# First layer of a graph network: the transposed one-hot rows made by ScalarE from destination numbers instead of turned by TensorE

## The reference, cut to what matters

```python
k = typed_linear(x, Wk, ntype, 3).reshape(n, H, D)      # q, v likewise
k_e = k[src]; v_e = v[src]; q_e = q[dst]
...
a = (kw * q_e).sum(-1) * pri[etype] / sqrt(D)            # 8 heads
attn = softmax of a over the edges of each dst
h = segment_sum(mv * attn[..., None], dst, num_segments=n)
h = typed_linear(h.reshape(n, H * D), Wa, ntype, 3)
x = layernorm(x + h * alpha + x * (1 - alpha))
# second layer: msg = (x @ weight[rel])[src] * norm * gate, summed by dst, relu, layernorm
```

## Time and profile before

| | us |
|---|---|
| median of 3 runs | 1799.43 (1798.69 to 1802.08) |
| the profiled execution | 1795.05 |
| its span | 1793.4 |
| PE busy | 1320.5 (74%) |
| DVE busy | 922.8 (51%) |
| POOL busy | 888.6 (50%) |
| ACT busy | 493.5 (28%) |

### The profile page before, as it was taken

The page is one execution under the profiler, slowest core; times in us unless marked ns, Lnnn a source line. Parts: engine busy times, 40 slices in busy tenths (PEclk is TensorE's granted clock), DMA queues, the critical chain, the costliest instruction groups (busy, mean ns, idle before and its releaser), DMA issues.

```text
span 1793.4 us, 21502 instructions
## 1 busy us (share of the span) xinstructions
PE 1320.5 (74%) x6758; PEld 1086.3 (61%) x6758; DVE 922.8 (51%) x1914; ACT 493.5 (28%) x1069; POOL 888.6 (50%) x905
## 2 busy tenths in 40 slices
PE   5789999558999999999999999932454444444445
PEld 4788888447878787878787878721233233233224
DVE  5734445457777777777777777320322222222222
ACT  3222322304454545454545454510000000000000
POOL 1041000375565656565656563057566666666662
PEclk9899999768999999999999999965566666666667
DMA  7454446565676767776767675343333333333332
GB/s 143 134 147 135 138 132 229 156 194 171 209 237 209 239 207 236 212 238 210 239 208 240 208 239 169 109 114 105 88 104 103 105 103 104 103 104 102 102 103 63
DMA packets 103851, 286.56 MB, mean 160 GB/s; under 512 B 20805, under 2 KB 40409, under 8 KB 100661
## 3 DMA queue, kind: packets, MB, share of 16 engines
q0 software_dynamic: 56032, 169.34, 31.9%
q1 hardware_dynamic: 47774, 116.71, 21.3%
HBM read 189.33 MB, written 96.65 MB: 159 GB/s over the span
## 4 chain that ended last, share of the span: by engine, by line
PE 57%; issue 24%; DVE 7%; DMA 6%; POOL 3%; ACT 1%; SPq 1%; another core or an unknown queue 1%; DVEq 0%; ACTq 0%; POOLq 0%
PE bank L954 15%; PE bank L837 11%; PE bank L865 10%; PE bank L729 5%; PE bank L795 5%; DMA kv_table<-tstage 4%; PE bank L783 2%; PE bank L751 2%; PE bank L737 2%; POOL kv L651 2%; PE bank L813 1%; DVE kv L1367 1%; DVE S L1372 1%; POOL kv L637 1%; PE bank L757 1%
## 5 line engine op out<-in xcount | busy, mean ns | idle before, releaser
L637 POOL DMA_INDIRECT kv<-kv_table,rows x416 | 457.8, 1101 | 306.6 <-PE bank L865 132.5
L651 POOL DMA_INDIRECT kv<-message_table,rows x416 | 394.8, 949 | 266.5 <-issue 122.8
L954 PE MATMUL bank<-kv,onehot_w 128*121 128x256 f32 x832 | 274.4, 462 | 334.1 <-issue 292.5
L954 PEld LDWEIGHTS bank<-kv,onehot_w 128*121 128x121 f32 x832 | 185.0, 224 | 423.6 <-issue 395.5
L837 PE MATMUL bank<-wr_r,x1T_r 128*121 128x512 f32 x1248 | 323.2, 401 | 2.2 <-ACT mstage L1098 2.2
L837 PEld LDWEIGHTS bank<-wr_r,x1T_r 128*121 128x121 f32 x1248 | 216.6, 183 | 51.4 <-ACT mstage L1098 3.4
L1504 DVE SCALAR_TENSOR_TENSOR z<-bank,xb 121x256 f32<-121x256 f32 x26 | 10.9, 418 | 414.9 <-remote 304.6
L1098 ACT ACTIVATE mstage<-bank,gate 121x256 f32<-121x256 f32 x416 | 171.4, 471 | 149.4 <-PE bank L837 133.6
L865 PE MATMUL bank<-kv,onehot_r 128*121 128x264 f32 x832 | 203.4, 393 | 0.0
L1176 ACT ACTIVATE sd<-mv,eps 121x1 f32<-121x1 f32 x26 | 7.7, 295 | 600.3 <-DVE mv L1510 513.4
L865 PEld LDWEIGHTS bank<-kv,onehot_r 128*121 128x121 f32 x832 | 150.9, 187 | 29.4
(11 more groups left out here) (135 smaller groups left out, 1396.7 us busy)
## 6 DMA issues: line engine op xcount, KB each, us to landing
message_table<-mstage SPq DMA_DIRECT2D x104, 484.0 KB
kv_table<-tstage SPq DMA_DIRECT2D x26, 1210.0 KB
kv<-kv_table,rows POOLq DMA_INDIRECT x416
kv<-message_table,rows POOLq DMA_INDIRECT x416
query_table<-qstage_r SPq DMA_DIRECT2D x26, 242.0 KB
qb_r<-query_table SPq DMA_DIRECT2D x26, 242.0 KB
kv<-in_Wr POOLq DMA_DIRECT2D x2, 2048.0 KB, 14.5
xb<-in_x SPq DMA_DIRECT2D x26, 121.0 KB
```

Source lines behind the costliest of these rows:

```text
L637: pool.indirect_dma_start(kv[:, n % 2, u, 0:2 * C], None, ktab, bass.IndirectOffsetOnAxis(ap=rows[:, 0, n, u:u + 1], axis=0)).then_inc(kv_ ...
L651: pool.indirect_dma_start(mrows[:, r.q, u, :], None, mtab, bass.IndirectOffsetOnAxis(ap=rows[:, 1, r.number, u:u + 1], axis=0)).then_inc(l ...
L954: last = mm(b_l[r.q][:NODES, 0:C], onehot_w[:, r.q, u, :], mrows[:, r.q, u, :], start=(u == 0), stop=(u == U - 1))
```

## The change

`onehotT_r` is no longer made from `onehot_r`. In every round SP reads the round's 2048 destination numbers, one line of 8 KB, into each of 121 partitions (`dsts`, 968 KB in all). For a group of four units ACT computes |destination - own node| in place (`apart`: Abs with a bias for each partition), and then relu(1 - that) into `onehotT_r` (`mark`), which is 1 where they agree and 0 elsewhere. The edges lie in `dsts` in memory order, so `onehotT_r` has its unit index innermost: the 128 columns of one unit's stationary operand are now 64 bytes apart, and each ACT operation takes 512 elements in runs of four. The 16 turns of a round on PE and the four ACT copies are gone.

```diff
                 onehot_r = msb("onehot_r", [P, 2, U, NODES], F32R)
-                onehotT_r = msb("onehotT_r", [NODES, U, P], F32R)
+                with ExitStack() as dst_life:
+                    dsts = sb("dsts", [NODES, P, U], I32, dst_life)
+                onehotT_r = msb("onehotT_r", [NODES, P, U], F32R)
...
+            def load_dst(r):
+
+                if not r.first:
+                    sp.wait_ge(qe_ready[1], r.nth(QB, 0))
+                s = sp.value_load(starts[0:1, bass.ds(r.number, 1)], min_val=0, max_val=E)
+                sp.dma_start(dsts[:, :, :].rearrange("n p u -> n (p u)"),
+                             dst_lines[0:1, bass.ds(s, ROUND_EDGES)].to_broadcast([NODES, ROUND_EDGES])
+                             ).then_inc(dst_landed, 16)
...
                 if not r.final:
                     load(r.next())
+                    load_dst(r.next())
...
-            def turn_onehot(r, g):
-                if g == 0:
-                    pe.wait_ge(oh_ready, r.done)
-                if g:
-                    pe.wait_ge(ohT_ready[g - 1], r.done)
-                else:
-                    wait(pe, ohT_ready[G - 1], r.number)
-                for q in range(GU):
-                    last = mm(b_ohT[:NODES, q * P:(q + 1) * P], onehot_r[:, r.par, g * GU + q, :], ident_r[:, :],
-                              start=True, stop=True)
-                last.then_inc(ohT_filled[g], 1)
...
-                            last = mm(b_qe[pr % 2][:, q * C:(q + 1) * C], onehotT_r[:, 2 * pr + q, :],
+                            last = mm(b_qe[pr % 2][:, q * C:(q + 1) * C], onehotT_r[:, :, 2 * pr + q],
...
-                    turn_onehot(n, 0)
                 messages(4)
                 if n:
-                    turn_onehot(n, 1)
                     hand_queries(n, 0)
...
-            def keep_onehotT(r, g):
-                act.wait_ge(ohT_filled[g], r.done)
-                a(onehotT_r[:, g * GU:(g + 1) * GU, :], b_ohT[:NODES, :].rearrange("p (a b) -> p a b", a=GU),
-                  ACT.Copy).then_inc(ohT_ready[g], 1)
+            def apart(r, g):
+
+                if g == 0:
+                    act.wait_ge(dst_landed, r.stores())
+                d = dsts[:, :, g * GU:(g + 1) * GU]
+                a(d.bitcast(F32), d, ACT.Abs, bias=minus_id[:NODES, bass.ds(r.number, 1)]
+                  ).then_inc(far_ready, 1)
+
+            def mark(r, g):
+                act.wait_ge(far_ready, r.nth(G, g + 1))
+                u = slice(g * GU, (g + 1) * GU)
+                a(onehotT_r[:, :, u], dsts[:, :, u].bitcast(F32), ACT.Relu, scale=-1.0, bias=1.0).then_inc(ohT_ready[g], 1)
...
                 messages(2)
+                if n:
+                    apart(n, 0)
                 messages(3)
                 if n:
-                    keep_onehotT(n, 0)
+                    mark(n, 0)
+                    apart(n, 1)
                 exps(r)
                 if n:
-                    keep_onehotT(n, 1)
+                    mark(n, 1)
```

More of the change, by code:

```diff
@@ L189, in build @@
         ident = sb("ident", [P, P])
-        ident_r = sb("ident_r", [P, P], F32R)
         iota_n = sb("iota_n", [P, NODES])
         base = sb("base", [P, ROUNDS])
+        minus_id = sb("minus_id", [P, ROUNDS])
         nmask = sb("nmask", [P, TILES, NT])
@@ L294, in build @@
         b_l = (bank[0], bank[1], bank[2], bank[4])
-        b_qe, b_ohT, b_agg, b_tmp, b_out, b_m = bank[0:2], bank[2], bank[3], bank[4], bank[5], bank[6:8]
+        b_qe, b_agg, b_tmp, b_out, b_m = bank[0:2], bank[3], bank[4], bank[5], bank[6:8]
         ld_grid, ld_x, ld_wa, ld_wr, ld_gw, ld_rel, ld_small, ld_rec = (sem(n) for n in (
@@ L303, in build @@
             "rel_high", "rel_low", "wr_high", "wr_low", "gw_high", "gw_low"))
-        const_ready, zeroed, rel_ready, ident_high = (sem(n) for n in (
-            "const_ready", "zeroed", "rel_ready", "ident_high"))
+        const_ready, zeroed, rel_ready = (sem(n) for n in ("const_ready", "zeroed", "rel_ready"))
         pool_step = sem("pool_step")
@@ L317, in build @@
         kv_landed = [sems(f"kv_landed{p}_", G) for p in range(2)]
-        ohT_filled, ohT_ready = sems("ohT_filled", G), sems("ohT_ready", G)
+        dst_landed, far_ready, ohT_ready = sem("dst_landed"), sem("far_ready"), sems("ohT_ready", G)
         qe_ready, qe_used = sems("qe_ready", 2), sems("qe_used", 2)
@@ L504, in l0 @@
                     store_x1(r.last())
+            load_dst(Round(sp, 0, 0))
             load(Round(sp, 0, 0))
@@ L598, in _ @@
             pool.iota(base[:, :], pattern=[[NODES, ROUNDS]], base=0, channel_multiplier=0,
+                      allow_small_or_imprecise_dtypes=True)
+            pool.iota(minus_id[:, :], pattern=[[-NODES, ROUNDS]], base=0, channel_multiplier=-1,
                       allow_small_or_imprecise_dtypes=True)
@@ L862, in aggregate @@
                 if g == 0:
+                    pe.wait_ge(oh_ready, r.done)
                     wait(pe, hN_ready, r.number)
@@ L896, in l0 @@
                 turn_back(r)
-                if n:
-                    turn_onehot(n, 0)
                 messages(4)
                 if n:
-                    turn_onehot(n, 1)
                     hand_queries(n, 0)
@@ L909, in l0 @@
                 if n:
-                    turn_onehot(n, 2)
                     hand_queries(n, 1)
@@ L914, in l0 @@
                 aggregate(r, 2)
-                if n:
-                    turn_onehot(n, 3)
                 aggregate(r, 3)
@@ L922, in _ @@
             first = Round(pe, 0, 0)
-            for g in range(G):
-                turn_onehot(first, g)
             for g in range(G - 1):
@@ L1012, in _ @@
             act.wait_ge(const_ready, 1)
-            a(ident_r[:, :], ident[:, :], ACT.Copy).then_inc(ident_high, 1)
             act.wait_ge(ld_gw, 16)
@@ L1141, in l0 @@
                     keep_x1T(f)
+                if n:
+                    apart(n, 2)
                 messages(5)
                 if n:
-                    keep_onehotT(n, 2)
+                    mark(n, 2)
+                    apart(n, 3)
                 if f:
@@ L1147, in l0 @@
                 if n:
-                    keep_onehotT(n, 3)
+                    mark(n, 3)
                 messages(6, 7)
@@ L1151, in _ @@
             for g in range(G):
-                keep_onehotT(Round(act, 0, 0), g)
+                apart(Round(act, 0, 0), g)
+                mark(Round(act, 0, 0), g)
                 if g % 2 == 0:
@@ L1353, in _ @@
             dve.wait_ge(x_low, STEPS * NX)
-            dve.wait_ge(ident_high, 1)
             v.memset(den[:, :], 1.0).then_inc(tables_over, 1)
```

## The result

| | us |
|---|---|
| before, median of 4 runs | 1799.06 (1797.53 to 1802.08) |
| after, median of 4 runs | 2025.66 (2022.81 to 2032.71) |
| ratio after / before | 1.1263, 95% interval 1.1244 to 1.1281 |
| forecast | 1909, range 1835 to 1985 |
| span of the profiled execution after | 2024.6 (before 1793.4) |

What follows compares the result with a forecast made beforehand. PE was taken to set the pace, with ACT's wait for the late `dsts` costing more than PE saves: 23 rounds at 3.2 and 1.2 us (74 + 28), plus 6 and 2, make 110; 1909 us, range 1835 to 1985.

Steps and rivals of the forecast that it cites:

- R: The beginning of a round on ACT's timeline; in the kernel before, rounds are 29.82 us apart.
- E: The start of `exps` on ACT; in the kernel before 12.49 us after R, with the next R 17.33 later.
- the case with nothing late: Rival: `dsts` lands in time for ACT, a round is 28.7 us, total 1775 to 1780; chance 0.08.
- I take R + 14.5, between them.: Landing of the `dsts` load, chosen between bounds R + 12.0 and R + 16.1; rounds 3.2 us longer.
- the upper bound, R + 16.1: Latest landing of `dsts`: 10.7 us, from the queue's 1.16 MB in 10 us with stores queued beside gathers.
- The estimate from the Trainium skill: 121 rows over 11 of 16 DMA engines: `dsts` takes 12 us, lands at R + 17.5, rounds 6.2 us more.
- I take the first for PE, since it is PE's own: PE's weight loads from columns 64 bytes apart cost nothing extra, by 8-column loads of 87 ns either way.
- The bound from ACT's row: Strided weight loads at ACT's 0.93 ns an element: 119 ns more a load, 2.85 us a round.
- The rival with both mechanisms: Late `dsts` load and dear strided weight loads on PE together: 66 us more, 1975 us; chance 0.22.
- E to the next round: From `exps` to the next round's beginning: 15.85 us instead of 17.33, DVE's products limiting PE's saving.
- 1.2 for the clock: PE's lower clock after its gap waiting for `mark`: 1.2 us a round, bounds 0 and 4.3.
- The cover: The store behind `dsts`, awaited by ACT's message 4: cost nothing while covered, 1 to 2 us a round otherwise.

Runs made afterwards that it cites:

- e9: Changed kernel with some data left out, `dsts` in its own buffer and loaded a round ahead, operand columns side by side, 121 partitions: 1796.83 us, 0.9990 of the kernel before.
- e8: Changed kernel with some data left out, `dsts` in its own buffer and loaded a round ahead, columns side by side, 128 partitions: 1781.67 us, 0.9891 of the kernel before.
- e4: Changed kernel with `dsts` read into 128 partitions instead of 121, all data computed: 1943.93 us, 1.0791 of the kernel before.
- e1: Kernel before, turns still on PE, with only the change's layout of `onehotT_r` (columns 64 bytes apart): 1877.17 us, 1.0423 of the kernel before.
- e6: Changed kernel with some data left out, `dsts` in its own buffer and loaded a round ahead, columns 64 bytes apart: 1827.30 us, 1.0143 of the kernel before.
- e5: Changed kernel with some data left out and `dsts` in its own buffer, load still late, columns 64 bytes apart: 2015.22 us, 1.1211 of the kernel before.
- e7: Changed kernel with some data left out and `dsts` in its own buffer, load still late, columns side by side: 2024.41 us, 1.1266 of the kernel before.
- e12: Kernel before, some data left out, plus the `dsts` load at the change's place ahead of the message stores, unused: 1976.49 us, 1.0976 of the kernel before.
- e3: Changed kernel with the `dsts` load issued ahead of the query and x rows: 1978.99 us, 1.0982 of the kernel before.
- e13: Kernel before, some data left out, plus the unused `dsts` load between the third and fourth message store: 1807.15 us, 1.0022 of the kernel before.
- e11: Kernel before, columns still side by side, but ACT's copy written in steps of 512 bytes: 1802.90 us, 1.0021 of the kernel before.

## Why the prediction failed

**Right.** The wait and its place, ACT at line 1053 ahead of message 3 with `exps` behind it, and the turns' removal lost in it. The issue at R + 5.4 was met to 0.1 us. `mark` took 626 ns against 634 forecast, `apart` 716. From the landing to `exps` 2.5 us passed (2.7). PE's busy share fell to 84% (some 80 forecast), its clock to 0.91. From E to the next R, with nothing late and the columns together, 15.85 us were worked out and e9 has 16.3. For the case with nothing late I had 1775 to 1780; e8 took 1781.67, but that is in part luck, since it leaves data out and has the columns together and 128 rows.

**Step that failed first: the landing.** "I take R + 14.5, between them." Measured R + 18.25 in the round above and R + 17.7 in the mean of rounds 3 to 23. Even the upper bound, R + 16.1, was below every one of these rounds. From issue to use I had bounds of 6.6 and 10.7 us; 128 rows stay within them (9.0 in e4), the 121 of the change don't (12.4). Both bounds came from transfers of another shape, and neither carried over. The estimate from the Trainium skill ("DMA: Bandwidth & Descriptors", the section on why a DMA increments its semaphore by 16), 12 us and R + 17.5, which the sum did without, was the nearest. The miss is 3.2 us a round. The first load, too, took longer than the 8.1 us assumed. Its issue and landing at the layer's start, 10.7 us apart, on SP's queue and on ACT:

```profile
342.20 0.38 SPq L493 DMA_DIRECT2D dsts<-in_dst_lines  x1
```

```profile
352.88 0.72 ACT L1053 ACTIVATE dsts<-dsts,minus_id 121x512 f32<-121x512 int32 x1 [21.58 <-DMA dsts<-in_dst_lines]
```

The layer begins 12.9 us later, where 6 were taken.

**Step that failed second: "I take the first for PE, since it is PE's own".** The row of PE's own load covers 8 columns, too few to show what 128 show. The bound from ACT's row was right almost to the number for a load: 119 ns more estimated, 122 measured in e1. Its 2.85 us a round, for three groups between E and the next R, were too much: at that place the columns cost 1.3 to 1.6 us (e6 to e9, e5 to e7). The rival with both mechanisms, at 1975, was the nearest case. That the columns were cheap was wrong, then, but with the load late it isn't shown to have cost the change anything: e7 has them together and is no faster than e5.

**E to the next round**, 15.85 and 1.2 for the clock forecast, 19.66 measured (853.20 to 872.86): 2.6 more; 19.3 and 2.3 more in the mean. I had DVE's products as what comes last, with group 2's sums at E + 7.7. They start at E + 10.65 (863.85), because PE comes late: queries, message 5 and the sums before them end at E + 8.2 (861.42) instead of E + 6.5. Both the slower loads and the lower clock are in that. The six message matmuls, 2.90 against 1.63, are 1.3 us of it, at a clock of 0.50, and have nothing to do with the columns. Nor have most of the first eight query matmuls, 2.16 us: with the columns together e7 has 2.07 for them. The second eight, 2.03 against 1.17 at a clock of 1.00, are the columns'. By the table of e5, e6, e7 and e9, the 15.85 were 0.5 too low, and the 1.2 for the clock, a guess between 0 and 4.3, 0.1 to 0.4; the columns, put at nothing, are the large part with 1.3 to 1.6.

**The sum.** 33.05 + 1.2 = 34.25 us a round forecast. 3.2 for the landing, 2.3 from E on and 0.2 less up to E make the 39.5 of rounds 3 to 23. Against the forecast that is 110 us in these 21 rounds. The first round begins 7 us later than was allowed for, and 4 us are lost behind the last round. Some 5 come off, since the forecast put 4.4 us between profile and median, where the profiled run after lies 0.6 above its median. That is, to 1 us, the 117 by which the forecast was short. e4 is a test of the sum with the landing nearly as it was put: used at R + 14.3, it still took 1943.93 us, 35 more than 1909. Its rounds 3 to 23 take 36.2 us, and what they have too much stands behind E (19.4 instead of 17.05). So some 80 us of the miss go with the landing and some 35 with what follows E.

**The cover.** "I cost it at nothing; with that cover gone it is 1 to 2 us a round." In the change the cover stands, so this is no part of the miss. But the price without it was wrong: 7.1 us a round in e12. A mend of the landing alone, without a word on the store behind it, can find this wait next, as e3 did; e4, with a shorter load and the same landing, has no such wait in its list.

## What to carry to other kernels

A large load costs by what it stands ahead of. Before placing one in a queue, list for each transfer behind it who waits for that and when: the same bytes cost 176 us ahead of a store that is waited for (e12) and 3 us behind it (e13). When a wait for a load goes, look for the second wait that it hid, and for the lower clock that the gap had brought. Don't take the price of a strided operand from a narrow instruction: here 8 columns showed nothing of what 128 cost, and the worse row of another engine was the better guess.

## What the runs showed of the hardware that was not expected

- A weight load of 128 fp32 columns from 121 partitions: 190 ns with columns side by side, 197 at 8 bytes from one to the next, 327 at 16, 312 at 64. With 8 columns it was 87 at 4 and at 64 bytes alike.
- 8 KB into each of 121 partitions took 11.0 to 13.7 us from issue to use (mean 12.4), into 128 partitions 7.9 to 10.0 from the same queue (mean 9.0) and 8.8 to 10.9 from another engine's (mean 10.0).
- With PE idle for 7.3 us in a round of the change, its granted clock was 0.50 for the 4.9 us behind the gap and 1.00 again 3.7 us later.
- ACT pays for writing in steps: 512 elements from a bank took 599 ns in order, 642 in pairs, 1098 in steps of 512 bytes; in e11 that cost the kernel 0.2%.
